# An attention loop on one core: causal masking of the exponentials by a GpSimd selection, with the weighting of values a step later, and other places for splits, loads and the output weight

## The reference, cut to what matters

```
scores = jnp.einsum('bihd,bjhd->bhij', q, k) * SCALE
causal = jnp.tril(jnp.ones((s, s), dtype=bool))
scores = jnp.where(causal, scores, jnp.finfo(scores.dtype).min)
attn = jax.nn.softmax(scores, axis=-1)
out = jnp.einsum('bhij,bjhd->bihd', attn, v)
out = out.reshape(b, s, NH * HD)
return out @ wo
```

## Time and profile before

| what | value |
|---|---|
| median of 3 runs | 1100.01 us (1099.08 to 1101.44) |
| the profiled execution, its own time | 1101.38 us |
| its span, first to last instruction | 1099.6 us |
| busy in the span | PE 953.8 us, DVE 703.6 us, ACT 537.1 us, POOL 203.1 us |
| granted TensorE clock, mean | 0.925 |

### The profile page before, as it was taken

The page is one execution under the profiler, slowest core; times in us unless marked ns, Lnnn a source line. Parts: engine busy times, 40 slices in busy tenths (PEclk is TensorE's granted clock), DMA queues, the critical chain, the costliest instruction groups (busy, mean ns, idle before and its releaser), DMA issues.

```text
span 1099.6 us, 14014 instructions
## 1 busy us (share of the span) xinstructions
PE 953.8 (87%) x5376; PEld 730.5 (66%) x5376; DVE 703.6 (64%) x877; ACT 537.1 (49%) x689; POOL 203.1 (18%) x200
## 2 busy tenths in 40 slices
PE   3793998987778579689899999999996999998996
PEld 1462565655445458577688888868885888886885
DVE  4632789875665667865775666535877867676652
ACT  1411556654443333354376555535772866665640
POOL 2000555554435621600000000000003000000003
PEclk9697899998887879879999999997998999998999
DMA  9276366563312021301053223212330233332202
GB/s 332 85 221 113 45 105 109 66 116 62 47 40 71 24 77 39 74 3 39 19 168 101 86 86 106 79 37 58 96 113 23 80 112 92 100 96 58 77 1 77
DMA packets 40019, 91.62 MB, mean 83 GB/s; under 512 B 6928, under 2 KB 10128, under 8 KB 39952
## 3 DMA queue, kind: packets, MB, share of 16 engines
q1 hardware_dynamic: 35072, 83.66, 30.6%
q10 hardware_dynamic: 4880, 7.07, 2.0%
HBM read 76.02 MB, written 2.10 MB: 71 GB/s over the span
## 4 chain that ended last, share of the span: by engine, by line
PE 58%; DVE 6%; issue 2%; ACT 2%; POOL 2%; POOLq 0%; ACTq 0%; DVEq 0%
PE PS L1370 12%; PE PS L1371 12%; PE PS L1372 12%; PE PS L1653 5%; PE PS L1654 5%; PE PS L1655 5%; PE PS L1573 1%; PE PS L1574 1%; POOL X L610 1%; PE PS L1639 1%; PE PS L1411 1%; DVE XN L996 1%; DVE SCR L1038 1%; PE PS L1629 1%; DVE ST L981 1%
## 5 line engine op out<-in xcount | busy, mean ns | idle before, releaser
L735 ACT ACTIVATE PL<-CODE 128x1024 f32<-128x1024 int32 x200 | 201.5, 1053 | 59.9 <-DVE ACC L1055 41.0
L1370 PE MATMUL PS<-HH,WRH 128*128 128x512 f32 x448 | 174.5, 390 | 0.0
L1372 PE MATMUL PS<-HL,WRH 128*128 128x512 f32 x448 | 174.3, 389 | 0.0
L1371 PE MATMUL PS<-HH,WRL 128*128 128x512 f32 x448 | 174.3, 389 | 0.0
L610 POOL TENSOR_TENSOR X<-X,SCR 128x512 f32<-128x512 f32 x32 | 42.7, 1342 | 663.4 <-DVE SCR L1038 663.2
L774 ACT ACTIVATE PT<-PS 128x512 f32<-128x512 f32 x160 | 86.0, 602 | 95.5 <-PE PS L1487 75.1
L1472 PE MATMUL PS<-KS,QS 128*128 128x128 f32 (+3 forms) x256 | 91.1, 437 | 47.2 <-DVE MX L1167 45.7
L1055 DVE SCALAR_TENSOR_TENSOR ACC<-PL,ACC 128x1024 f32<-128x1024 f32 x100 | 124.8, 1248 | 9.7 <-ACT PL L735 1.5
L626 POOL TENSOR_TENSOR QS<-ident,MX 64x256 fp32r<-64x256 f32 x128 | 94.7, 740 | 112.8 <-DVE MX L1167 106.0
L1167 DVE TENSOR_REDUCE MX<-PS 128x2 f32<-128x256 f32 (+3 forms) x128 | 99.9, 818 | 21.9 <-PE PS L1474 14.2
L1318 DVE TENSOR_TENSOR HID<-SG,PS 128x512 f32<-128x512 f32 x56 | 38.2, 684 | 112.6 <-PE PS L1574 67.6
(11 more groups left out here) (228 smaller groups left out, 1702.1 us busy)
## 6 DMA issues: line engine op xcount, KB each, us to landing
CODE<-in_CODES SPq DMA_DIRECT2D x50, 512.0 KB, 3.6
SCALE<-in_SCALES SPq DMA_DIRECT2D x100, 256.0 KB, 4.3
WM<-in_WM SPq DMA_DIRECT2D x12, 1024.0 KB, 7.0
QS<-FH SPq DMA_DIRECT2D x32, 128.0 KB, 4.1
QS<-FL SPq DMA_DIRECT2D x32, 128.0 KB, 5.2
X<-in_X ACTq DMA_DIRECT2D x2, 1024.0 KB, 12.1
out_x<-X ACTq DMA_DIRECT2D x8, 256.0 KB, 2.0
WF<-in_LBGU SPq DMA_DIRECT2D x14, 128.0 KB, 2.1
```

The costliest lines, as they stand in the source:

```text
L735: nc.scalar.activation(PL[:, n % 3], CODE[:, p % 2], ACT.Prelu, scale=scale, bias=bias, alpha=alpha).then_inc(s_plane, 1)
L1370: nc.tensor.matmul(dst, lh, rh, start=start and k == 0, stop=False)
L1371: nc.tensor.matmul(dst, ll, rh, start=False, stop=False)
L1372: ins = nc.tensor.matmul(dst, lh, rl, start=False, stop=stop and k == KC - 1)
```

## The change

It has these parts.

1. `transposed(n)` loses its mask product. Instead POOL sets the upper triangle of the diagonal block's exponentials to zero in a new helper, `cut(n)`, an in-place `affine_select` over 128 x 512 values, and `weighted(n)` waits for the cut (`s_tri`) where it reads that block. POOL runs `cut(n - 3)` at the end of unit n, behind scaling and adding, and waits for its end. The scores for the maxima keep their mask.
2. PE issues the weighting one step later: at every odd n, `weighted(n - 5)` and `weighted(n - 4)`.
3. Pieces 0 and 1 are loaded behind the stack of group 0 in place of group 2.
4. Rounding and splitting of finished pairs go by two tables, `ROUND_AT` and `SPLIT_AT`. Only pairs 0 to 3 are split in the loop; pairs 4 to 6 are split behind it.
5. `WOH` is rounded after the exponentials of unit 62. Its splitting moves from POOL to DVE, right behind the maxima. Three tiles have other addresses for this.
6. The wait for the last copy moves from ahead of the gates to the one `wo` product that needs bank 7. DVE copies the gates earlier, and the load of `LDA` is issued later.

```diff
-PIECES_AT = {2: (0, 1), 5: (2,), 7: (3,), 10: (4,), 12: (5,)}
+PIECES_AT = {0: (0, 1), 5: (2,), 7: (3,), 10: (4,), 12: (5,)}
-SPLIT_AT = {40: 0, 44: 1, 48: 2, 52: 3, 58: 4, 60: 5, 62: 6}
+ROUND_AT = {41: 0, 46: 1, 49: 2, 54: 3, 58: 4, 60: 5, 62: 6}
+SPLIT_AT = {46: 0, 51: 1, 54: 2, 59: 3}
...
+            def cut(n):
+
+                block = block_of(n, n % TB)
+                pool.wait_ge(s_exp, STC(n // TB) + (n % TB + 1) * (n % TB + 2) // 2)
+                nc.gpsimd.affine_select(block[:], block[:], [[0, REP], [1, P]], ALU.is_ge, 0.0, base=0,
+                                        channel_multiplier=-1).then_inc(s_tri, 1)
+                pool.wait_ge(s_tri, n + 1)
...
                 if n in add_at:
                     add_half(*add_at[n])
-            pool.wait_ge(s_w0h, 1)
-            nc.gpsimd.tensor_tensor(WOL[:], WOF[:], WOH[:], ALU.subtract).then_inc(s_w0l, 1)
+                if n >= 3:
+                    cut(n - 3)
+            for n in range(B * GROUPS * TB - 3, B * GROUPS * TB):
+                cut(n)
...
-                if n in SPLIT_AT:
-                    round_heads(*divmod(SPLIT_AT[n], PAIRS))
-            act.wait_ge(s_wo, 16 * REP)
-            act.wait_ge(s_pv, B * GROUPS * TB)
-            nc.scalar.activation(WOH[:], WOF[:], ACT.Copy).then_inc(s_w0h, 1)
+                if n in ROUND_AT:
+                    round_heads(*divmod(ROUND_AT[n], PAIRS))
+                if n == units - 2:
+                    act.wait_ge(s_wo, 16 * REP)
+                    nc.scalar.activation(WOH[:], WOF[:], ACT.Copy).then_inc(s_w0h, 1)
...
-                if n - 1 in SPLIT_AT:
-                    split_heads(SPLIT_AT[n - 1])
+                if n in SPLIT_AT:
+                    split_heads(SPLIT_AT[n])
 
             last = B * PAIRS - 1
+            dve.wait_ge(s_st, STC(B * GROUPS - 1))
+            dve.wait_ge(s_w0h, 1)
+            nc.vector.tensor_tensor(WOL[:], WOF[:], WOH[:], ALU.subtract).then_inc(s_w0l, 1)
+            for pair in range(PAIRS, last):
+                split_heads(pair)
             copy_odd(last)
+            gates("ga0")
...
-                                           QS[:, q % STACKS, :, ic * P:(ic + 1) * P], start=True, stop=jc < ic)
-                    if jc == ic:
-                        ins = nc.tensor.matmul(dst, maskB[:], identB[:].unsqueeze(1).to_broadcast([P, REP, P]),
-                                               start=False, stop=True)
+                                           QS[:, q % STACKS, :, ic * P:(ic + 1) * P], start=True, stop=True)
...
-                    pe.wait_ge(s_exp, blocks[1])
+                    if jc < ic:
+                        pe.wait_ge(s_exp, blocks[1])
+                    else:
+                        pe.wait_ge(s_tri, n + 1)
...
-                if n >= 3 and n % 2 == 0:
-                    for unit in (n - 4, n - 3):
+                if n >= 5 and n % 2 == 1:
+                    for unit in (n - 5, n - 4):
                         weighted(unit)
             pe.wait_ge(s_mx, 2 * units)
-            pe.wait_ge(s_odd, 2 * B * PAIRS)
```

More of the change, by code:

```diff
@@ L265, in build @@
         ATF = sb("ATF", [P, KC, D], F32, dec0 + 8 * K)
-        BTF = sb("BTF", [P, KC, D], F32, dec0 + 16 * K)
-        WOH = sb("WOH", [P, KC, D], F32R, R0 + 48 * K)
-        WOL = sb("WOL", [P, KC, D], F32R, R0 + 56 * K)
+        BTF = sb("BTF", [P, KC, D], F32, dec0 + 24 * K)
+        WOH = sb("WOH", [P, KC, D], F32R, dec0 + 16 * K)
+        WOL = sb("WOL", [P, KC, D], F32R, R0 + 92 * K)
         ATH = sb("ATH", [P, KC, D], F32R, R0 + 64 * K)
@@ L352, in build @@
         s_exp = sem("exponentials_ready")
+        s_tri = sem("diagonal_blocks_cut")
         s_pv = sem("values_weighted")
@@ L767, in _ @@
             done = 0
-            for n in range(B * GROUPS * TB):
+            units = B * GROUPS * TB
+            for n in range(units):
                 ic = n % TB
@@ L781, in _ @@
                     fold(step_at(n)[0])
-                if n in SPLIT_AT:
-                    round_heads(*divmod(SPLIT_AT[n], PAIRS))
-            act.wait_ge(s_wo, 16 * REP)
-            act.wait_ge(s_pv, B * GROUPS * TB)
-            nc.scalar.activation(WOH[:], WOF[:], ACT.Copy).then_inc(s_w0h, 1)
+                if n in ROUND_AT:
[3 more added lines that the diff above has]
+                    nc.scalar.activation(WOH[:], WOF[:], ACT.Copy).then_inc(s_w0h, 1)
             round_heads(B - 1, PAIRS - 1)
-            act.dma_start(LDA[:], a["LDA"]).then_inc(s_ldw, 16)
             act.wait_ge(s_wf, N_QKV)
@@ L799, in _ @@
             act.wait_ge(s_mm, J["wo", NT - 1] + 1)
+            act.dma_start(LDA[:], a["LDA"]).then_inc(s_ldw, 16)
             act.wait_ge(s_wf, N_QKV)
@@ L1191, in _ @@
             split_heads(last)
-            gates("ga0")
             gated(("wo", 0))
@@ L1507, in weighted @@
                 ins.then_inc(s_pv, 1)
-            for n in range(units + 3):
+            for n in range(units + 4):
                 if n < units:
@@ L1525, in _ @@
                     pe.wait_ge(s_oL, PAIRS * (t // TB + 1))
+                if bank(("wo", t)) == 7:
+                    pe.wait_ge(s_odd, 2 * B * PAIRS)
                 product(begin(("wo", t)), f_cols(slice(t * P, (t + 1) * P)), pair(WOH, WOL, slice(0, D))
```

## The result

The changed kernel takes 1127.6 us (1127.3 to 1127.7, four runs) against 1100.1: a ratio of 1.0248, 95% interval 1.0231 to 1.0266. It is slower by 27.4 us. The forecast was 1112 with a range of 1078 to 1130: the sign and the range held, but the loss is more than twice the 12 us that were forecast.

The account below looks back on a forecast made before the run. PE and DVE were taken to share the limit, about 24.5 us per 8 units, with stalls at three places. 1101.4 less gains of 48.4 plus costs of 60 (19 + 8 + 21 + 5 + 3 + 4) gave 1112 us; range 1078 to 1130.

Parts of the forecast that it names:

- Start 14.4: Start: codes issued 22 us earlier, so maxima of unit 1 begin near 95.0, not 109.38; 14.4 us gained.
- The other two, 27.3 and 6.7: Loop's waits for rounding go, 27.3 us gained; at the end WOH is ready before the last weighting ends, 6.7 gained.
- Sum 27.7: A block of 8 units lengthens from 24.5 to 27.7 us; 3.2 lost in each of six whole blocks, 19 together.
- Behind it on ACT stand two copies and a curve: Queue behind ACT's late copy_even, copies, curves and exponentials: 6.3 us before PE can finish transposed(n + 3).
- the term of 3 for two curves at n % 8 == 7: Blocks with two curves there (units 23 and 55) have 1.0 to 1.9 us more on ACT: 3 us cost.
- of which the 1.05 wait goes since nothing is weighted just ahead of those scores: Maxima 11 to the end of maxima 15, 14.3 us before: its 1.05 wait goes, leaving 13.25.
- So I add 4: Clock 0.85 in the stretch with stalls against 1.00 in the quiet one; PE idling some 8 us a block: 4 us cost.
- the terms for folds and further steps: Cuts behind folds at units 10, 18, 34, 42, 50: 21 us; POOL steps at 19, 35, 43, 51: 5.
- nothing by itself: Removing PE's 64 mask products of 0.38 us, 24 us of PE, counted as no gain; DVE works 22.1 of 24.6 us.
- The late copies are mostly hidden: Rival, chance 0.31: ACT can catch up, blocks stay at 24.5 us; 1081 us, or 1060 if POOL keeps up at folds.
- The cut is dear: Rival, chance 0.13: at 1.8 us a cut POOL needs the whole block's time; 1127 us, range 1124 to 1145.
- No difference: Rival, chance 0.06: errors in gains of 48 and costs of 60 cancel; 1100 us, within 0.2%.

Follow-up runs that it names:

- experiment 1: Changed kernel with the mask product back, no cut and the weighting at its old steps; parts 3 to 6 kept: 1051.5 us.
- Experiment 2: Changed kernel with the mask product back in place of the cut; weighting still one step late: 1108.8 us.
- experiment 5: Changed kernel with the mask product back in place of the cut, weighting late, both bank 7 copies (ACT's, DVE's) one unit later: 1067.4 us.
- experiment 10: Changed kernel with cut(n - 3) at the start of POOL's unit n, ahead of diagonal and scaling; weighting still late: 1110.9 us.
- experiment 8: Changed kernel with weighting at its old steps and neither mask product nor cut, so the exponentials' diagonal blocks are unmasked: 1048.6 us.

## Why the prediction was right and wrong

The whole account, by medians: parts 3 to 6 gain 48.6 us (48.4 forecast), the late weighting costs 57 (34 forecast: 19 + 8 + 3 and the clock's 4), the cuts cost 19 (26 forecast). 1100.1 - 48.6 + 57 + 19 = 1127.5. Two errors of opposite sign stand in it: 23 us too little for the weighting, 7 too much for the cuts. With the first alone the time would have been 1135, above the range of 1078 to 1130, so that the range held is in part luck.

**Gains.** "Start 14.4": it is 14.7 in experiment 1 (maxima of unit 1 at 94.72) and 15.75 after. The other two, 27.3 and 6.7, can't be read apart, since part of the waits for rounding lay behind unit 59. From the maxima of unit 11 to the first output product, before took 204.5 us (140.59 to 345.11) and experiment 1 takes 172.9 (126.08 to 298.96): 31.6 for 34.0; another 1.7 came behind it without a forecast. Together, right.

**The late copies: the step that was mis-sized.** The mechanism was right, and so were its marks: both copies wait, the curves come late, the wait at the copy is 3 to 4 us. The size was not. Experiment 2 has the late weighting alone; where it loses its time against experiment 1, by the profiled executions (us):

| stretch | forecast | measured |
|---|---|---|
| up to the maxima of unit 11 | 3 | 6.8 |
| six blocks | 19, curves 3, clock 4: 26 | 38.8 (189.1 against 150.3) |
| from the maxima of unit 59 to the first output product | 5 | 8.6 |
| behind it | 0 | -2.9 |
| sum | 34 | 51.2 (by the medians 57) |

So the step that failed is "Sum 27.7", the length of a block, from which the 19 us come. The blocks are 30.2, 31.1, 31.4, 33.3, 30.5 and 32.6. Link by link:

| link | forecast | blocks from the maxima of 11, 19, 27, 35, 43, 51 | over the forecast, all six |
|---|---|---|---|
| maxima of 11 to the end of those of 15 | 13.25 | 14.6, 13.3, 14.4, 15.0, 15.2, 14.8 | 7.8 |
| from there to the maxima of 18 | 8.2 | 8.9, 11.0, 9.9, 11.6, 8.6, 11.1 | 11.9 |
| maxima, wait, copies | 6.27 | 6.7, 6.7, 7.1, 6.7, 6.7, 6.8 | 3.2 |
| curves that ACT makes in the second link | 2 | 2, 4, 3, 3, 2, 4 | |

The second link is the largest miss. "Behind it on ACT stand two copies and a curve [...] a curve": those are two curves, and only the blocks of 11 and 43 have two. Where ACT has three or four curves of some 0.95 us there, the link takes 9.9 to 11.6; the term of 3 for two curves at n % 8 == 7 covers a part of it. The longest, 11.6, has three curves as the one of 9.9 has, and the same 70 products, but at a granted clock of 0.71 for 1.00 PE is busy 9.7 us in it for 7.5.

The first link has a saving that did not come: "of which the 1.05 wait goes since nothing is weighted just ahead of those scores". The six first links are 87.3 us here and 87.2 in experiment 1. In five blocks of six a wait for scores stands one unit earlier instead, at the maxima of units 14 (1.26 us at 142.60 above), 30, 38, 46 and 54, 1.0 to 1.6 us each; step 13, and every eighth behind it, now weights just ahead of these scores. But the block of 19 has the same order and no such wait. Its first link has a clock of 1.00, where the block of 11 has 0.88, but the block of 51 has 1.00 too and waits 1.55. So neither the order nor the clock makes the wait by itself, and its cause stays open. What experiment 5 shows is that a late weighting costs 9 us of waiting for scores, within 16 of time, even where both copies have been moved out of its way. In the sum it was nothing. The third link has 0.38 for the mask product that the changed kernel lacks.

The clock is the other term that was too small. Experiment 2, block 35 to 43:

```profile
225.54:258.84 33.30, 27.48 (x252) 17.33 (x252) 21.09 (x25) 16.10 (x27) 14.47 (x19) 0.85 0.50 80
```

The same 252 products take PE 27.5 us here and 25.1 in the first block at 0.94, and 22.3 in a block of experiment 1 at 1.00. "PE would idle some 8 us a block" was right: 208.1 less PE's 159.4 in the six blocks after is 8.1 each. "So I add 4" was not. The granted clock of these six blocks is 0.74 to 0.86 after, 0.81 on the mean, where the stretch with stalls that served as the measure had 0.85, and the six blocks hold 23 us more of PE's time than in experiment 1 (159.4 against 135.9). How much of this lies on the path wasn't tested alone, since no experiment changes the clock and nothing else; it stays open.

**The cuts: right, a little too dear.** 19 by experiment 2 and the kernel after, 16.7 by experiment 10, for 26 forecast. A cut of 0.654 for 0.9 on 17 of them would have made it 4 less. The places were right: 6.06 to 7.42 us at units 10, 18, 42 and 50. Block by block the kernel after is 2.6, 1.9, 4.2, 5.0, 4.3 and 1.0 us over experiment 2, where the terms for folds and further steps give 3.1, 1.25, 6.5, 5.55, 4.35 and 1.25: unit 34, at 6.5 forecast as the dearest, has 4.2, and the longest block is not its own (35.6) but the next (38.3). A weighting behind such a cut, PE's timeline after:

```profile
168.63 0.45 PE L1522 MATMUL PS<-PT,V 128*32 128x128 f32 x8 [2.60 <-POOL PT L626]
```

and POOL's, with the scaling and the cut that it waited for:

```profile
166.61 1.26 POOL L584 TENSOR_TENSOR WT<-ACC,SCALE 128x512 f32<-128x512 f32 x1 [2.09 <-issue]
167.94 0.63 POOL L626 TENSOR_SCALAR_AFFINE_SELECT PT<-PT 128x512 f32<-128x512 f32 x1
```

The fold ended at 166.5 on ACT, then scaling, then cut, then the eight products, then DVE's copy at 169.13.

**The mask product, "nothing by itself": right,** as far as experiment 8 can tell. The reason given, that DVE has nearly a block's time of work, fits, but wasn't tried by making DVE's work shorter.

**The rivals.** "The late copies are mostly hidden" fell by experiments 2 and 5. "The cut is dear" had the time that came, 1127, but not the reason: a cut is 0.654 us, and not 1.8. "No difference" and "the codes come no earlier" fell by the result and by the start.

## What to carry to other kernels

When a producer is moved a step later, every in-order consumer that was placed for its old step has to be moved too. Here the copies that weren't moved cost 41 us, far more than either the producer's move or the operation for whose sake it was made. Look at what is queued behind each waiting consumer: DVE's copy held the maxima, ACT's copy the curves, and both in turn PE. And 24 us of PE's work, taken away with the weighting at its old place, gave nothing clear of the noise: price what is taken off a busy engine by what waits for it there, not by its busy time.

## What was not expected of the hardware

The stage behind the loop gained 5.5 us, though little of it was changed. Its first 115 us in the kernel before, 397 products in two windows:

```profile
345.10:406.00 60.90, 40.83 (x172) 32.27 (x172) 36.64 (x59) 18.47 (x22) 31.26 (x16) 0.78 0.25 77
406.00:460.00 54.00, 49.88 (x225) 40.11 (x224) 43.61 (x108) 19.26 (x28) 16.51 (x10) 0.97 0.14 40
```

and the same stretch after, 398 products in 109.5 us:

```profile
376.50:437.00 60.50, 40.82 (x190) 32.76 (x190) 45.81 (x88) 19.39 (x25) 27.78 (x14) 0.86 0.26 78
437.00:486.00 49.00, 44.59 (x208) 35.77 (x207) 39.85 (x83) 18.20 (x25) 16.25 (x10) 1.00 0.15 43
```

The granted clock is 0.86 and 1.00 in them for 0.78 and 0.97. The output products show it one by one. Before, they began 0.43 us apart:

```profile
345.70 0.63 PE L1371 MATMUL PS<-WOH,FL 128*128 128x512 f32 x1
346.13 0.63 PE L1372 MATMUL PS<-WOL,FH 128*128 128x512 f32 x1
```

and after 0.23 apart, about the ratio of the two levels, 1.2 and 2.4 GHz:

```profile
376.82 0.39 PE L1389 MATMUL PS<-WOH,FL 128*128 128x512 f32 x1
377.05 0.40 PE L1390 MATMUL PS<-WOL,FH 128*128 128x512 f32 x1
```

Ahead of these products before, PE stood idle for 2.37 us behind POOL's splitting; after, it has small products right up to them. That is not enough for it, though. Experiment 1 has the same code behind the loop as the kernel after; its output products begin 0.23 apart too, but those from 300.31 to 303.30 are 0.43 apart, and from the first of them to the end of the span it takes 752.8 us, for 749.0 after and 754.5 before. Why the chip grants one level here and the other there, the runs do not settle. It is only read that blocks with more idle time of PE have slower products as well (27.5 us for 252 of them at 0.85, 22.3 at 1.00), and that some of a loss in the loop can come back in a later stage.
